# A block with a mixture of experts on one core: 39 slots that always run in place of 40, six behind the branch in place of five

## What is computed

```python
def ffn(h, router_w, w1, b1, w2, b2):          # h: layer norm of the tokens
    x = h.reshape(-1, 256)
    logits = x @ router_w                       # 4096 x 14
    assignments = argmax(logits, axis=-1)
    weights = softmax(logits)[assignments]
    hid = gelu(einsum('nd,edf->nef', x, w1) + b1)   # 14 experts, 512 hidden
    all_out = einsum('nef,efd->ned', hid, w2) + b2
    return all_out[assignments] * weights       # added to the tokens
```

## Time and profile before

| what | value |
|---|---|
| median of the 3 timed runs | 509.92 us |
| lowest and highest of them | 509.88 and 630.88 us |
| the profiled execution: its span, from its first to its last instruction | 518.2 us |
| its own time beside the span | none is given |
| mean granted TensorE clock in it | 0.992 |
| slots that ran in it | 40 (640 matmuls of L1520) |

### The profile page before, as it was taken

One profiled execution on the slowest core, in us unless ns is written; L12 is line 12 of the kernel. 1 busy time (PEld: TensorE's weight loads), 2 busy tenths in 40 slices (PEclk: granted clock), 3 DMA queues, 4 the chain that ended last, 5 costly groups with the idle time before them and its releaser, 6 DMA issues.

```text
span 518.2 us, 14215 instructions
## 1 busy us (share of the span) xinstructions
PE 495.9 (96%) x4278; PEld 397.8 (77%) x4279; DVE 335.8 (65%) x1027; ACT 335.0 (65%) x814; POOL 246.1 (47%) x432
## 2 busy tenths in 40 slices
PE   8999999999999999999999999999879999999992
PEld 6545554667888888888888887778769999999992
DVE  4476665657889999888988899984632333323231
ACT  3766666589888988888888888764523333343430
POOL 2468665354334664655556555625443233333332
PEclk9999999999999999999999999999989999999998
DMA  8959995500002223222221122174545766666520
GB/s 302 311 173 282 304 259 172 168 1 3 2 2 72 67 74 92 92 51 88 92 92 46 46 63 69 44 250 145 183 167 186 220 208 209 220 192 212 187 82 8
DMA packets 35681, 70.41 MB, mean 136 GB/s; under 512 B 6752, under 2 KB 22242, under 8 KB 35632
## 3 DMA queue, kind: packets, MB, share of 16 engines
q1 hardware_dynamic: 31744, 60.72, 38.7%
q0 software_dynamic: 3456, 8.85, 4.5%
q10 hardware_dynamic: 432, 0.26, 0.2%
HBM read 58.93 MB, written 11.61 MB: 136 GB/s over the span
## 4 chain that ended last, share of the span: by engine, by line
PE 82%; DVE 5%; issue 4%; ACT 3%; POOL 2%; another core or an unknown queue 2%; DMA 1%; DVEq 0%; SPq 0%; POOLq 0%; ACTq 0%
PE psum L1520 11%; PE psum L1533 10%; PE psum L1446 9%; PE psum L1425 6%; PE psum L1404 6%; PE psum L1412 5%; PE psum L1475 5%; PE psum L1272 5%; PE psum L1372 5%; PE psum L1334 3%; PE psum L1343 3%; PE psum L1291 3%; PE psum L1294 3%; PE psum L1347 3%; PE psum L1312 2%
## 5 line engine op out<-in xcount | busy, mean ns | idle before, releaser
L1520 PEld LDWEIGHTS psum<-arena,ring 128*128 128x128 f32 x640 | 77.5, 192 | 4.6 <-ACT arena L1205 2.2
L1520 PE MATMUL psum<-arena,ring 128*128 128x128 f32 x640 | 78.5, 276 | 1.6 <-ACT arena L1205 1.5
L1533 PE MATMUL psum<-w_s,arena 128*128 x320 | 77.5, 386 | 0.0
L1205 ACT ACTIVATE arena<-psum 128x256 f32<-128x256 f32 x40 | 15.4, 385 | 94.0 <-PE psum L1272 53.0
L1021 DVE TENSOR_TENSOR arena<-psum,tok 128x256 f32<-128x256 f32 x40 | 17.0, 425 | 90.1 <-PE psum L1533 83.0
L1533 PEld LDWEIGHTS psum<-w_s,arena 128*128 128x128 f32 x320 | 58.7, 193 | 6.8
L545 POOL TENSOR_TENSOR ov<-o_n,v_s 128x256 f32<-128x256 f32 x32 | 26.1, 816 | 77.1 <-DVE o_n L785 77.1
L1171 ACT ACTIVATE arena<-kT,head_mask 128x256 f32<-128x256 f32 x128 | 59.3, 532 | 0.0
L603 POOL DMA_INDIRECT out<-arena,token_of x40 | 39.8, 996 | 19.7 <-POOL token_of L595 14.5
L1211 ACT ACTIVATE arena<-psum,b_s 128x128 f32<-128x128 f32 x160 | 45.6, 375 | 3.8 <-PE psum L1520 2.2
L892 DVE TENSOR_REDUCE smax<-psum 128x16 f32<-128x1024 f32 x32 | 39.1, 1222 | 11.4 <-PE psum L1425 11.3
(11 more groups left out here) (206 smaller groups left out, 1093.5 us busy)
## 6 DMA issues: line engine op xcount, KB each, us to landing
ring<-w SPq DMA_DIRECT2D x40, 512.0 KB, 3.6
w_s<-ctxT SPq DMA_DIRECT2D x15, 768.0 KB, 8.9
w_s<-w SPq DMA_DIRECT2D x16, 448.0 KB, 3.4
slot_rec<-routed SPq DMA_DIRECT2D x40, 132.0 KB
tok<-x SPq DMA_DIRECT2D x16, 256.0 KB, 8.2
w_s<-xT SPq DMA_DIRECT2D x12, 256.0 KB, 6.0
routed<-pad_rec SPq DMA_DIRECT2D x1, 1980.0 KB, 8.9
tok<-b SPq DMA_DIRECT2D x14, 128.0 KB
```

What stands on the lines that cost most here:

```text
L1520: mm = pe.matmul(hid_bank(p)[:, f * P:(f + 1) * P], w1_s[:, r, c * F + f * P:c * F + (f + 1) * P], xgT[:, p, c * P:(c + 1) * P], start=c = ...
L1533: mm = pe.matmul(bank(2 + q, D), hidT[:, q, f * P:(f + 1) * P], w2_s[:, bass.ds(e * (FC * D) + f * D, D)], start=f == 0, stop=f == FC - 1)
```

## The change

EVEN is 39, the expected number of slots (32 tiles and half a slot for each of 14 experts), where it was that number rounded up to a multiple of four. The end of the hardware loop was EVEN - 4; it is now LOOPED, the largest number of whole passes of eight that leaves at least one of the always-run steps outside: 11 + 1 + (39 - 11 - 2) // 8 * 8 = 36. The branch is taken where more than 39 slots are used, and its body holds slots 39 to 44.

```diff
-EVEN = -(-(NTOK // P + E // 2) // 4) * 4
+EVEN = NTOK // P + E // 2
...
 HEAD = -(-(HEADT * P - E * (P - 1)) // P)
 LOOSE = 7
 RECS = 8
+LOOPED = HEAD + 1 + (EVEN - HEAD - 2) // RECS * RECS
...
 def run_slots(engine, step, first, last, used_tab, begin=0):
-    run_steps(engine, lambda i, k: step(i, k, (0, EVEN)), begin, EVEN + last, HEAD + 1, EVEN - 4, RECS)
+    run_steps(engine, lambda i, k: step(i, k, (0, EVEN)), begin, EVEN + last, HEAD + 1, LOOPED, RECS)
     used = engine.value_load(used_tab[0:1, 0:1], min_val=0, max_val=NSLOT)
     with engine.If(used > EVEN):
         for i in range(EVEN + first, NSLOT + last):
             step(i, i % RECS, (EVEN, NSLOT))
```

## The result

| | median of all runs | lowest to highest |
|---|---|---|
| before, 6 runs | 510.16 us | 509.88 to 630.88 |
| after, 6 runs | 506.86 us | 506.20 to 508.52 |

The ratio is 0.9932 with an interval of 0.9917 to 0.9946, so 2.8 to 4.2 us less; like all ratios here it goes by fast runs alone, and so without the one of before that took 630.88 us. The forecast was 506.2 us, the range 505.0 to 508.0.

A forecast was written before the change was run, and what follows sets the result against it. TensorE, without gaps in the expert stage, was taken to bound the kernel. One slot less gave -3.73 us and all other terms 0, so 509.92 became 506.2 us, range 505.0 to 508.0.

The forecast's parts named there:

- Step 1: Expert stage: one slot of TensorE work goes, priced at the full slot distance, 3.73 us less.
- the branch isn't taken: End of the always-run slots: 38 slots in use, one below the new bound, so slot 39's padding is no longer run.
- Step 2: Hardware loop's end: the new expression still gives 36, three passes of eight as before; cost 0.
- Step 3: Slot 39's two DMA loads, first matrix and records, go; TensorE doesn't wait for such loads, so they give nothing.
- Step 5: SP's wait for the last four writes moves from step 39 to 38, covered 4.1 us by POOL's drain; cost 0.
- Step 4: Used-slots read, compare and branch over a body one slot longer: 0, with 0.5 us either way for an instruction load.
- Step 6: POOL's last writes before its final drain: drain seems to have its own length, about 6.0 us; 0, at most 1 more.
- The rival in which the tail takes a part back: Kernel's end: drain waits for real bytes or the jump loads twice; 1 to 2 us, say 507.7 us; chance 0.08.
- The sum: Whole kernel: -3.73 us against the profiled span, 518.2 to 514.5 us, carried unchanged to the timed median of 509.92.
- the signs: Expected in the later profile: last first layer near 499.85, POOL's drain from about 508.3, span about 514.5 us.
- The rival on the other side: Branch at the end taken with 40 slots in use: 45 slots run, 33 us more, about 543 us; chance 0.02.

The follow-up runs named there:

- run 45: Not a label of a run: the words say that inputs using more than 40 slots make either kernel execute 45 slots.

## Why the prediction was right

**Step 1, the slot, is right to 0.01 us.** 3.73 us were forecast from the distance in the earlier trace rows; 3.72 us went, and EVEN = 38 and 44 have the same price for each slot, down and up. The slot behind a turn back of the loop, 3.86 us in the prediction, was read at one turn only; at the other, 432.2 us in the same trace, it is 3.88. No term used it. The reason is what the stretch with 12.00 us of 12.00 showed: with one engine full and all others waiting for it, the price of a unit of work is its distance on that engine.

**That the branch isn't taken is right.** It was read from 0.00 MB in the packets of two writes. After, the packets of the last write hold none and those of the write before it hold 0.07 MB; these windows are 497 to 499 and 499 to 501 us of the kernel after:

```profile
q0 software_dynamic: 48, 0.07, 9.7%
```

```profile
q14 instruction: 1, 0.01, 1.8%
q0 software_dynamic: 48, 0.00, 1.6%
```

**Step 2** (the loop's end costs nothing) is right, and had it moved by a pass, it would have been 0.23 us. **Step 3** is right: the stretch per slot doesn't change with the loads. **Step 5** is right, with 3.9 us of cover left.

**Step 4** took 0 with 0.5 us either way. POOL's branch to drain is 0.48 us in both kernels, so 0 is right. Of the upside at most a third is there to be had: where the jump was short, the tail was 0.16 us shorter than the change's once (loop to 28) and 0.17 us longer than that of before once (EVEN = 44). In both the drain began while the issue of the last write still ran, and counted from the end of that issue it took 5.89 and 6.30 us. By the rule that the prediction takes from the Trainium skill, Advanced Engine Details and Errata, "ISA Cache", a body one slot longer could have brought one instruction load more. On POOL none came: one load of 8 KB (queue 14) stands by the jump after as it did before, here from 498.8 to 499.5 us.

```profile
q14 instruction: 1, 0.01, 4.5%
```

In the two kernels with the short jump none stands there. That the load is what makes the jump long isn't shown: in the kernel without slot 38's write it starts only when the drain does, and branch to drain is 0.48 us all the same. On TensorE the jump took 2.51 and 2.03 us in the two kernels with EVEN = 38. In both, a load of 16 KB (queue 8) begins 0.3 us ahead of the jump; where it took 0.21 to 0.45 us, none begins within a microsecond of it. This is the one with EVEN = 38 alone, 491 to 494.5 us:

```profile
q8 instruction: 1, 0.02, 2.6%
```

This fits a jump that waits for a load, but it wasn't tested.

**Step 6** is right, and its reason (the drain has a length of its own) went from a guess to something that two kernels show. The rival in which the tail takes a part back is out: the tail gave 0.08 us. Those 0.08 us are the drain itself, 6.03 us and then 5.95, a term that the prediction doesn't have.

**The sum** was against a profile of the wrong kind. I took the 8.3 us by which the timed median lies under the profiled span for something constant. It isn't: the time of an execution is 1.8 us above its span, and the first profile was of one some 10 us longer than usual. This did no harm because all the surplus lay ahead of slot 8, outside the stretch from which the steps were read. The forecast of 506.2 us was worked out from the timed median, so the wrong span cancels in it; what it spoiled are the absolute times of the signs. The page alone could have raised the question, since its span lies above all timed runs of before but one.

**The rival on the other side** was priced at about 543 us for 40 used slots. With EVEN = 37 the same working, 6 slots and 14.6 us, gave 544 and the chip 544.12. The total agrees in part by luck, as its parts were off against each other: the gap was 17.23 us and not 18.3, and the slot behind it, at half clock, was 0.95 us longer than 3.73.

**What the change costs on other inputs.** No input with 40 used slots was run, but its price can be worked out from the runs: 6 slots (22.4 us) and the emptying (15.0 us) on a kernel that is 3.8 us shorter, 33.6 us above before. So the change pays only if 40 comes up less than about once for every nine times of 39 or fewer. By the reference's routing for 33 drawings of its inputs (seeds 0 to 32), 17 use 39 or fewer, 10 use 40 and 6 use more, which run 45 slots in either kernel. It wins on the input that is timed and would lose over drawn ones. A cheaper branch alone doesn't turn that: with emptying at 4.0 us the price is 22.6 us, and ten times that is still over three times what 17 gains of 3.8 us give, since most of it is six slots of which one is used.

**The median** moved by 3.3 us in one measurement and 3.8 in the other, around the 3.80 that the profiles have. What lies between is the start.

## What to carry to other kernels

With one engine full, cutting a unit of work is worth its distance on that engine, and a padded unit is as dear as a full one. A bound like EVEN should be set by the distribution of what is used and the two prices, not by the mean alone, and before it is lowered the branch should be made cheap: a wait that belongs to the end of the kernel shouldn't stand ahead of it (15.0 us became 4.0), and a body that runs only the slots in use would save more (an estimate of five slots, 18.7 us, with 40 in use; no run has it).

## What was not expected of the hardware

- POOL's drain at the end of the program takes 5.87 to 6.03 us where it starts behind the end of the last write's issue, also with all writes landed (5.88 us, 0.15 us behind a branch). The longer ones, 6.11, 6.51 and 7.58 us, began while that issue still ran. The one of 7.58 us, from the kernel that takes the branch:

```profile
535.45 0.97 POOL L604 DMA_INDIRECT out<-arena,token_of  x1 [0.72 <-issue]
```

```profile
L124 POOLq DRAIN  x1: 7575/7575/7575, 535.2 to 535.2; - x1
```

- Counted from the later of its start and the end of that issue, the drain takes 5.87 to 6.38 us in all twelve profiles. It is longest where most padding slots stand at the end: 6.38 us with seven, 6.30 with six, 6.03 with two, 5.87 to 5.95 with one or none. Why isn't shown. It is two thirds of the 9 us behind the last finish. SP's drain takes 0.01 to 0.09 us.
- From the finish of slot 7 to the end, the two profiles of before agree to 0.01 us, and so do the two of after. Up to there eleven of the twelve profiles lie within 2.8 us, and one lies 7 to 10 us behind them.
- The jump over the branch's body took TensorE 0.35 us with EVEN = 40, 0.45 with 39 (0.36 with the loop ended at 28), 2.51 and 2.03 with 38 and 0.21 with 44, where VectorE took 0.06 and POOL 0.05 each time.
